# Edge loop of a graph network kernel: GpSimd waits for layer 4, three groups on, ahead of each group's gathers

## What is computed

```python
rbf = jnp.exp(-0.5 * ((d[:, None] - centers) / (jnp.abs(widths) + EPS_W)) ** 2)
r = rbf * env[:, None]
r = _silu(r @ rbf_w1 + rbf_b1) @ rbf_w2 + rbf_b2
W = _silu(r @ filt_w1 + filt_b1)
W = _silu(W @ filt_w2 + filt_b2) @ filt_w3 + filt_b3
msg = (x[col] @ node_w + node_b) * W
agg = jax.ops.segment_sum(msg, row, num_segments=x.shape[0])
h = x + agg
```

## Time and profile before

| what | value |
|---|---|
| median of three runs | 5700.58 us (5696.37 to 5717.07) |
| the profiled execution's own time | 5722.47 us |
| its span, first to last instruction | 5720.7 us |
| busy: PE, VectorE (DVE), ScalarE (ACT), GpSimd (POOL) | 3678.5, 2387.8, 1607.6, 3435.5 us |
| edge loop, about | 140 to 2660 us of the span |

### The profile page before, as it was taken

One profiled execution on the slowest core, in us unless ns is written; L12 is line 12 of the kernel. 1 busy time (PEld: TensorE's weight loads), 2 busy tenths in 40 slices (PEclk: granted clock), 3 DMA queues, 4 the chain that ended last, 5 costly groups with the idle time before them and its releaser, 6 DMA issues. The chain is left out here.

```text
span 5720.7 us, 76061 instructions
## 1 busy us (share of the span) xinstructions
PE 3678.5 (64%) x16356; PEld 2722.4 (48%) x16357; DVE 2387.8 (42%) x7105; ACT 1607.6 (28%) x4212; POOL 3435.5 (60%) x3664
## 2 busy tenths in 40 slices
PE   7888888888888888888998433333332454444443
PEld 5555555555555555555887323222222444444443
DVE  5444444444444444443326322122212654545557
ACT  4444343444434434344666211111110000000000
POOL 2655555655555656565764666666666566666665
PEclk8888889888888988899999666665655777776776
DMA  7333333333333333334994111111112333333324
GB/s 221 110 107 106 108 109 106 109 107 105 109 109 105 108 106 110 106 110 146 297 293 135 54 43 44 45 43 43 44 44 60 101 86 87 84 82 86 87 79 91
DMA packets 460153, 590.18 MB, mean 103 GB/s; under 512 B 65456, under 2 KB 380848, under 8 KB 460080
## 3 DMA queue, kind: packets, MB, share of 16 engines
q0 software_dynamic: 128512, 318.04, 18.3%
q1 hardware_dynamic: 331584, 271.50, 16.8%
HBM read 392.61 MB, written 197.07 MB: 103 GB/s over the span
## 5 line engine op out<-in xcount | busy, mean ns | idle before, releaser
L533 POOL DMA_INDIRECT s_rows<-arena,adr x784 | 790.0, 1008 | 809.5 <-issue 765.9
L573 POOL DMA_INDIRECT d_rows<-arena,adr x832 | 810.0, 974 | 503.7 <-issue 250.0
L586 POOL DMA_INDIRECT arena<-x_half,idx x832 | 801.7, 964 | 503.4 <-issue 227.8
L525 POOL DMA_INDIRECT arena<-y_rows,idx x784 | 757.3, 966 | 306.0 <-issue 238.2
L987 PE MATMUL ps<-f3s,arena 128*128 128x256 f32 x3136 | 878.2, 442 | 40.5 <-issue 40.4
L1375 DVE TENSOR_TENSOR arena<-arena,ps 128x512 f32<-128x512 f32 x392 | 268.0, 689 | 1354.0 <-remote 611.7
L987 PEld LDWEIGHTS ps<-f3s,arena 128*128 128x128 f32 x3136 | 720.7, 230 | 185.3 <-issue 47.9
L1164 PE MATMUL ps<-arena 128*128 128x128 f32 x1664 | 372.3, 393 | 663.3 <-DVE arena L1557 586.8
L976 PE MATMUL ps<-arena,f2s 128*128 128x512 f32 x1568 | 732.2, 611 | 30.9 <-ACT arena L640 29.2
L1164 PEld LDWEIGHTS ps<-arena 128*128 128x128 f32 x1664 | 321.1, 288 | 704.9 <-issue 703.9
L647 ACT ACTIVATE arena<-ps,col 128x512 f32<-128x512 f32 x392 | 268.1, 684 | 1009.1 <-PE ps L976 840.5
(11 more groups left out here) (217 smaller groups left out, 5444.2 us busy)
## 6 DMA issues: line engine op xcount, KB each, us to landing
arena<-s_rows SPq DMA_DIRECT2D x104, 1048.0 KB, 5.7
arena<-d_rows SPq DMA_DIRECT2D x52, 1040.0 KB
arena<-de_rows SPq DMA_DIRECT2D x392, 128.0 KB
d_rows<-arena,adr POOLq DMA_INDIRECT x832
arena<-x_half,idx POOLq DMA_INDIRECT x832
s_rows<-tpl_s SPq DMA_DIRECT2D x98, 131.0 KB
arena<-y_rows,idx POOLq DMA_INDIRECT x784
s_rows<-arena,adr POOLq DMA_INDIRECT x784
```

Source lines behind the costliest of these rows:

```text
L525: pool.indirect_dma_start(gath[b][:, t, :], None, y_rows, bass.IndirectOffsetOnAxis(ap=idx[b][:, t:t + 1], axis=0)).then_inc(gathered[b], 16)
L533: pool.indirect_dma_start(s_rows, bass.IndirectOffsetOnAxis(ap=adr[b][:, t:t + 1], axis=0), msg[b][:, t, :], None).then_inc(scattered[b], 16)
L573: pool.indirect_dma_start(d_rows, bass.IndirectOffsetOnAxis(ap=adr2[b][:, t:t + 1], axis=0), drow[b][:, t, :], None).then_inc(scattered_d[ ...
L586: pool.indirect_dma_start(gath2[b][:, t, :], None, x1_half, bass.IndirectOffsetOnAxis(ap=idx2[b][:, t:t + 1], axis=0)).then_inc(gathered2[ ...
```

## The change

Ahead of the gathers of group g+4, and behind the scatters of group g, GpSimd waits until `l4_mm` has reached 2(g+3) + 2, that is until both halves of layer 4 of group g+3 are done. The first four groups have no such wait, and the last four have no gathers.

```diff
--- before.py
+++ after.py
@@ -541,6 +541,9 @@
             def exchange(g, q, b):
                 if ahead(g, 4):
                     scatter(g, q, b)
+
+                    if not (fixed(g) and g < 4):
+                        hold(pool, l4_mm, 2 * (g + 3) + 2)
                     gather(g + 4, q + 1, b)
                 else:
                     scatter(g, q, b)
```

## The result

The changed kernel takes 5780.98 us in the median (5764.36 to 5797.44, 4 runs) against 5704.9 us (5696.37 to 5717.07, 4 runs) of the kernel before: a ratio of **1.0136, 95% interval 1.0118 to 1.0153**. The prediction had said 5630 us and faster; the time lies in its range, and the direction that came is that of its rival C. The profiled execution took 5764.36 us around a span of 5762.6, so 42 us over the span of before.

A forecast was written before the change was run, and what follows sets the result against it. GpSimd's chain was taken as the bound at 13.18 us a group, PE's updates being held beside gathers; 1.2 + 10.1 + 1.5 = 12.8 us over 188 groups saves 71 us, giving 5630 us; range 5260 to 5850.

The forecast's parts named there:

- rival C: GpSimd's wait for layer 4: slower by long holds, 5830 us if one group in three is struck; chance 0.23.
- The bound, and who waits for whom: Edge loop: PE's semaphore updates are held while GpSimd issues gathers; the chain closes on GpSimd at 13.34 us, 13.18 measured.
- Order and place: GpSimd in the edge loop: gathers move some 9 us, scatters follow 0.30 us behind, then the pause; nobody waits for landings.
- The cycle of 12.8 us: New GpSimd period: 1.2 us wake-up, 10.1 us burst, 1.5 us until layer 4's update is seen.
- The saving of 71 us: Edge loop: 188 groups, each going from 13.18 to 12.8 us.
- rival A: Edge loop: scatters hold no updates, period 10.3 us, floor 5180 us, or 5290 us at 11.0 us; chance 0.24.
- the upper bound: New cycle: layer 4's update, ending inside the burst, is held until GpSimd stops; gives the 1.5 us term.
- The rows of ScalarE: Kernel before, near 1012 us: layer 4's first half seen at 1014.83, its second only at 1024.46, after the following burst.
- the tail's evidence: End of kernel: eight scatters run without a pause, yet the second product starts 0.2 us late at most after layer 5.
- the turning point: Slower case: the sign turns when the pause of 5.9 us, 3.2 us over forecast, strikes more than one group in eight.
- The eleven gaps under 0.6 us: Between gathers and scatters, groups 10 to 186: each is followed two groups on by a hold of 4 to 10 us.
- Rival B: Edge loop: nothing gained, as updates come free with the scatters' landing or the lag is PE's own; 5700 us, chance 0.15.

The follow-up runs named there:

- The pause experiments: Changed kernel plus a GpSimd iota and a wait for its end between each group's scatters and the layer 4 wait: 5459.59 us, 0.9689 of the kernel before.
- the hold one group earlier: Changed kernel with the added wait on layer 4 of group g+2 instead of g+3: 4687.29 us, 1.0006 of the kernel before on that chip.

## Why the prediction was wrong

- **The bound, and who waits for whom**: right. PE's updates are held beside GpSimd's rows of DMAs, and the period closes on GpSimd. The pause experiments changed nothing but GpSimd's gaps, and took the delays over 8 us from 138 to 1. By whom the updates are held is not shown.
- **Order and place**: right for the groups in which the wait is late. Gathers, then scatters 0.3 us behind them, the pause before the gathers, landings waited for by nobody. The idle time moved as said.
- **The cycle of 12.8 us**: right for the median group, 12.77 us. The saving of 71 us is there (74 by the counts), if each cycle were of that length. That layer 4 ends 3.45 us after it starts is a small misreading: rows 4 have 3.60, which moves rival A's period by less than 0.1 us.
- **The step that failed** is the upper bound that I took in the part on the new cycle: layer 4's update "is held until GpSimd stops", so that in the sum each burst starts behind a pause of 2.7 us. Updates are held often, not always. Work that ends inside a burst is sometimes seen in time (1032.37 above), and then the new wait is satisfied before GpSimd reads it, in 35 of the 183 groups from 8 to 190. The rows of ScalarE held both cases, a first half that ended at 1012.98 and was seen 1.85 us later, beside running scatters, and a second half held for 9.8 us, and I argued from the second alone. I also had the tail's evidence that updates pass beside scatters, and used it only for rival A as a whole, never group by group. The two cases mix within one run, and it is the mixture that hurts.
- **What it did to the sum**: I forecast a saving of 0.38 us in each group. The term left out is 54 us for 35 joined bursts and 69 us for longer pauses around them. The pauses over 5 us are theirs: all but a few follow a row of 16 directly or with one burst between.
- **Rival C** had the place (the wait for layer 4 on GpSimd), the price (3.2 us for a pause of 5.9 instead of 2.7) and the turning point (one group in eight) right: 40 pauses over 5 us in some 181 groups is one in 4.5, and 12.8 + 3.2/4.5 = 13.5 us, against 13.40. Its cause, that gathers beside layers 1 and 5 make longer holds, is not what the trace shows; it didn't name the joined bursts, so that its number is right in part by luck. Its counter-argument, that the next burst "can't start until layer 4 is seen, which itself gives the pause that frees the updates", is the same error again, and kept its chance at 0.23. The eleven gaps under 0.6 us in the kernel before, each with a hold behind it, were the sign to follow: the edit lets exactly such a gap, of 0.30 us, occur when its wait is early.
- **Rival A** fell on the chips that hold updates. On the other one the kernel before runs at about A's period, but there the gathers hold nothing either. **Rival B** fell as far as a lag of PE's own goes: its 5700 us was nearer than my 5630, but the cycle's parts all moved, and with a pause of 2.13 us the long delays are gone. Whether the updates come free with a landing no run here decides.

## What to carry to other kernels

A wait is no pause: where engines gain because another one falls silent for a while, a wait that can be early, as here, gives that silence in some iterations and joins two bursts in others, so ask of each added wait what happens when it is already satisfied. If silence is what is wanted, make it unconditional and measure its least length; here 2.13 us in each group gave 3.1% less time than before and 5.0% less than the changed kernel (5459.59 against 5748.22 us on the same chip). Try such a thing on more than one chip, for on the one that held nothing the same pause cost 7.4%.

## What the chip did that I had not expected

- **One chip took 17 to 18% less time for this kernel.** The kernel before took 4683.33 us there, and 5631.78 to 5716.54 us in the medians of the other sets, with 0.2 to 0.5% between the lowest and the highest run of a set. In the edge loop the difference is how soon PE's updates are seen beside indirect DMAs: from its first scatter to its last the changed kernel with the pause takes 2334 us on that chip and 2335 on the other, where the kernel without one (the hold one group earlier there, the kernel before here) has 1987 and 2561. Of the 422 us that the two spans with the pause still differ by, 418 lie in the scatter and gather stages behind the loop, which have no pause (1069 against 1251 us, and 1055 against 1290). That held updates are the cause there too is argued from these rows alone. In the scatter stage ScalarE's copy and VectorE waited for a source that the profile can't name in the changed kernel (waits, 3200 to 4150 us: total, times, longest),

```profile
DVE arena L1503 <- remote: 686.2, 59, 22.6
ACT arena L783 <- remote: 686.0, 59, 19.4
```

  and on the other chip, in the kernel with the hold one group earlier (2600 to 3400 us), VectorE's same line waits for DMAs, 4.0 us at the most:

```profile
DVE arena L1503 <- DMA d_rows<-arena,adr: 587.8, 157, 4.0
```

- **Held updates come free by 2.0 us after GpSimd's last indirect DMA instruction ends**, 155 of 242 between 1.4 and 2.0, when the pause is 2.13 us.
- **The clock adds to each long hold.** The 8 matmuls of layers 2 and 3 took 1.14 us at 1032.27 and 2.08 us at 1049.90, after PE had been idle for 7.02 us; the 8 of layer 4 took 3.60 us and, after 6.20 us of idle time, 6.49. The granted clock is 1.00 from 1032.27 to 1033.40 and 0.50 from 1049.90 to 1052.00 in the first trace, and 0.56 from 1052.40 to 1058.80 in the second: the two levels are 2.4 and 1.2 GHz. The slices say the same: 8 and 9 in the loop of the changed kernel, 9 all through with the pause, and the mean matmul of layer 4 went from 636 to 594 ns.
